# Normalisations written out over one buffer, and one product and one state moved in a state-space scan

## The reference

```python
x = x + _L2_attn_a_ref(_layernorm(x, axis=-1), ...)
x = x + _L2_ffn_ref(_layernorm(x, axis=-1), ...)
```

```python
q = jnp.where(signatures_raw > 0.3, 1.0, jnp.where(signatures_raw < -0.3, -1.0, 0.0))
sigs = signatures_raw + jax.lax.stop_gradient(q - signatures_raw)
cluster_sigs = jnp.sign(sigs.reshape(NUM_CLUSTERS, TPC, D).mean(axis=1))
```

## Time and profile before

| what | value |
|---|---|
| median of three runs | 5309.79 us |
| the profiled execution, its own time | 5316.4 us |
| its span, first to last instruction | 5314.5 us |
| PE, DVE, ACT, POOL busy | 69%, 65%, 44%, 34% |
| mean granted TensorE clock | 0.812 |

### The profile page before, as it was taken

One profiled execution on the slowest core, in us unless ns is written; L12 is line 12 of the kernel. 1 busy time (PEld: TensorE's weight loads), 2 busy tenths in 40 slices (PEclk: granted clock), 3 DMA queues, 4 the chain that ended last, 5 costly groups with the idle time before them and its releaser, 6 DMA issues. The chain is left out here.

```text
span 5314.5 us, 74791 instructions
## 1 busy us (share of the span) xinstructions
PE 3686.4 (69%) x21578; PEld 2430.3 (46%) x21578; DVE 3452.9 (65%) x6649; ACT 2334.0 (44%) x4251; POOL 1781.2 (34%) x1703
## 2 busy tenths in 40 slices
PE   5757566588873568873577777479936949577595
PEld 4657346533322423333422322246634649555494
DVE  4422671379996368854389999668866647656575
ACT  2335324355541347761444444347634526343253
POOL 0043114456661445552234445102220132301423
PEclk9868668789996789995778888679966869778697
DMA  2022002212220232300311111000000012100122
GB/s 96 2 60 78 12 3 83 81 56 64 64 66 13 80 91 88 90 25 28 109 45 49 52 48 56 9 19 1 1 3 2 0 33 61 54 9 0 35 67 61
DMA packets 263352, 238.41 MB, mean 45 GB/s; under 512 B 32713, under 2 KB 217136, under 8 KB 262176
## 3 DMA queue, kind: packets, MB, share of 16 engines
q1 hardware_dynamic: 242592, 193.03, 12.1%
q0 software_dynamic: 20480, 41.98, 2.5%
HBM read 159.06 MB, written 74.97 MB: 44 GB/s over the span
## 5 line engine op out<-in xcount | busy, mean ns | idle before, releaser
L1987 DVE TENSOR_TENSOR_SCAN s_l_attn_a_h<-s_l_attn_a_da,XN 128x512 f32<-128x512 f32 x512 | 598.3, 1210 | 54.9 <-issue 35.3
L1937 ACT ACTIVATE s_l_attn_a_da<-s_l_attn_a_delta,s_l_attn_a_a 128x510 f32<-128x510 f32 x512 | 346.2, 686 | 557.6 <-DVE s_l_attn_a_h L1987 554.3
L1929 PE MATMUL s_l_attn_a_y_ps<-XN,c_ident 128*128 128x512 f32 x1024 | 552.9, 664 | 36.5 <-DVE s_l_attn_a_y L2259 28.9
L611 POOL DMA_INDIRECT s_l_ffn_ffn_back<-slots_y,s_l_ffn_ffn_slots x320 | 304.5, 952 | 515.7 <-DMA slots_y<-PICK 259.8
L507 DVE COPY s_l_ffn_ffn_xt<-s_l_ffn_ffn_turned 128x128 f32<-128x128 f32 x416 | 120.3, 290 | 534.8 <-PE s_l_ffn_ffn_turned L663 532.8
L603 POOL DMA_INDIRECT slots_x<-XN,s_l_ffn_ffn_slots x320 | 309.7, 968 | 451.9 <-DVE s_l_ffn_ffn_slots L482 213.1
L438 ACT COPY s_l_ffn_ffn_own_w<-up 128x512 f32 (+2 forms) x416 | 304.9, 734 | 297.8 <-DVE s_l_ffn_ffn_expert_no L491 193.2
L1947 POOL TENSOR_TENSOR XN<-s_l_attn_a_h,LOG 128x512 f32<-128x512 f32 x256 | 319.8, 1272 | 316.3 <-DVE s_l_attn_a_h L1987 299.8
L674 PE MATMUL s_l_ffn_ffn_up<-s_l_ffn_ffn_xt,s_l_ffn_ffn_own_w 128*128 128x128 f32 x2944 | 412.6, 281 | 6.5 <-DVE s_l_ffn_ffn_shifted_a L515 5.4
L682 PE MATMUL s_l_ffn_ffn_down<-down,s_l_ffn_ffn_hid 128*128 x2944 | 407.4, 279 | 12.9 <-DVE s_l_ffn_ffn_hid L520 6.0
L1947 POOL TENSOR_TENSOR XN<-s_l_attn_a_h,s_l_attn_a_more_c_rows 128x512 f32<-128x512 f32 x256 | 321.0, 1275 | 250.9 <-DVE s_l_attn_a_h L1987 158.2
(11 more groups left out here) (655 smaller groups left out, 8259.7 us busy)
## 6 DMA issues: line engine op xcount, KB each, us to landing
LOG<-s_l_attn_a_c_kept SPq DMA_DIRECT2D x128, 256.0 KB, 3.1
s_l_attn_a_more_c_rows<-s_l_attn_a_c_kept SPq DMA_DIRECT2D x128, 256.0 KB, 3.1
XNT<-slots_x SPq DMA_DIRECT2D x64, 320.0 KB, 5.0
slots_y<-LOG SPq DMA_DIRECT2D x16, 640.0 KB, 4.4
slots_y<-PICK SPq DMA_DIRECT2D x16, 640.0 KB, 4.4
s_l_attn_b_qr<-s_l_attn_b_q_rows SPq DMA_DIRECT2D x64, 144.0 KB
s_l_attn_b_kr<-s_l_attn_b_k_rows SPq DMA_DIRECT2D x64, 144.0 KB
XNT<-slots_x SPq DMA_DIRECT2D x16, 384.0 KB, 4.9
```

Source lines behind the costliest of these rows:

```text
L611: nc.gpsimd.indirect_dma_start(back[:, n % 8, :], None, k.slots_y[h][0:NH * P, :], bass.IndirectOffsetOnAxis(slots[:, c, t:t + 1], 0)).the ...
L1929: last = self.nc.tensor.matmul(self.y_ps[:, i, :], self.k.ident[:], self.hc[n % 2][:, i, :], start=(n == 0 and not begun), stop=(n == NST ...
L1937: self.nc.scalar.activation(self.da_half(g, n, i)[:, :, 1:], self.delta[par][:, i, :].rearrange("p (b t) -> p b t", b=BPG)[:, :, 1:], ACT. ...
L1987: self.nc.vector.tensor_tensor_scan(self.h[n % 2][:, i, :], self.da_half(g, n, i).rearrange("p b t -> p (b t)"), self.u[n % 2][:, i, :], 0 ...
```

## The change

- **Normalisation.** All loops are written out. VectorE writes rows directly into `XN`, so that neither a ring nor GpSimd's copy is needed. ScalarE makes one copy per group, to `XNT`, and the projection reads its weights there. There are three `turned` banks (and three `proj` banks for 72 columns). TensorE's order becomes turn(g+2), project(g). With 8 columns the logits of four groups share a bank and are copied at once. Where statistics are still to be taken, the work goes in three chunks of 8, 8 and 16 tiles. ScalarE loads the table that the next block needs at g = 2.
- **Signatures.** `SIG` is built once, in the first block of the program.
- **Scan of layer 2.** `spread_lam` is one product of two rows: the tile `lam` gets a second row of ones. `project_dt` goes from 12 to 11, `spread_mean` and `move_c` from 14 to 13, `keep_ssm` from 11 to 10, `keep_z` from 12 to 11, `sizes` from 14 to 12, `log_term` from 15 to 14.

```diff
 def load_all(nc, k, weights):
+        raw, q, low = s.sb("raw", [P, NT]), s.sb("q", [P, NT]), s.sb("low", [P, NT])
             sp.dma_start(k.X[:], k.dram["x"]).then_inc(loaded, 16)
+            sp.dma_start(raw[:], k.dram["L2f_sig"]).then_inc(sig_loaded, 16)
...
+            dve.wait_ge(sig_loaded, 16)
+            nc.vector.tensor_scalar(q[:], raw[:], 0.3, None, ALU.is_gt)
...
+            def normalise(g):
+                for t in range(g * GT, (g + 1) * GT):
+                    last = nc.vector.tensor_scalar(k.XN[:, t, :], k.X[:, t, :], meanvar[:, t, 0:1], rstd[:, t:t + 1], ALU.subtract, ALU.mult)
+                last.then_inc(rows_ready, 1)
+            if stats_taken:
+                find_moments(0)
+                invert(0)
+                for g in range(GROUPS):
+                    normalise(g)
+            else:
+                take(0, 2 * GT)
+                find_moments(0)
+                take(2 * GT, 4 * GT)
+                find_moments(1)
+                invert(0)
+                normalise(0)
+                normalise(1)
+                take(4 * GT, 6 * GT)
+                invert(1)
+                normalise(2)
+                take(6 * GT, TILES)
+                find_moments(2)
+                normalise(3)
+                invert(2)
+                for g in range(4, GROUPS):
+                    normalise(g)
...
+            turn(0)
+            turn(1)
+            for g in range(GROUPS):
+                if g + 2 < GROUPS:
+                    turn(g + 2)
                 if project is not None:
+                    project_rows(g)
...
+            for g in range(GROUPS):
+                act.wait_ge(turned_ready, g + 1)
+                nc.scalar.copy(k.XNT[:, g * GROUP:(g + 1) * GROUP], turned[g % 3][:]).then_inc(cols_ready, 1)
+                if g == 1 and len(chunks) == 3:
+                    root(2)
+                if g == 2 and project is not None:
+                    nc.scalar.preload_act_table_set("sigmoid_and_others" if wide else "natural_log_exp_and_others")
...
 def l2_attn_a
             def spread_lam(q):
-                nc.tensor.matmul(aux[:, 0, :], half_row[LAM:LAM + 1, :], k.ones[LAM:LAM + 1, 0:1].to_broadcast([1, GROUP]), start=True, stop=False)
-                nc.tensor.matmul(aux[:, 0, :], half_row[LAM:LAM + 1, :], lam[LAM:LAM + 1, :], start=False, stop=True).then_inc(lam_up, 1)
+                nc.tensor.matmul(aux[:, 0, :], half_row[LAM:LAM + 2, :], lam[LAM:LAM + 2, :], start=True, stop=True).then_inc(lam_up, 1)
...
-                    if n == 12 and r < GROUPS:
+                    if n == 11 and r < GROUPS:
                         project_dt(r)
-                    if n == 14:
+                    if n == 13:
                         if r < GROUPS:
                             spread_mean(r)
                         move_c(q)
...
+            nc.gpsimd.memset(lam[LAM:LAM + 2, :], 1.0)
...
-                        if n == 12:
+                        if n == 11:
                             keep_z(q)
                     if r < GROUPS:
-                        if n == 11:
+                        if n == 10:
                             keep_ssm(r)
+                        if n == 12:
+                            sizes(r)
                         if n == 14:
-                            sizes(r)
-                        if n == 15:
                             log_term(r)
...
 def l2_ffn
-    with Scope(nc, name + "_sig") as s:
...
-            sp.dma_start(raw[:], k.dram["L2f_sig"]).then_inc(loaded, 16)
...
-    layer_norm(nc, k, name + "_ln", k.SIG, NS, keep_rows=True)
+    layer_norm(nc, k, name + "_ln", k.SIG, NS)
```

More of the change, by code:

```diff
@@ L200, in _, with take, find_moments @@
         def _(dve):
-            if not stats_taken:
-                for t in range(TILES):
+            def take(first, last):
+                for t in range(first, last):
                     nc.vector.bn_stats(stats[:, t, :], k.X[:, t, :])
+            def find_moments(c):
+                some = slice(*chunks[c])
                 dve.drain()
-            nc.vector.tensor_tensor(meanvar[:, :, 0], stats[:, :, 1], stats[:, :, 4], ALU.add)
-            nc.vector.tensor_tensor(half_gap[:], stats[:, :, 1], stats[:, :, 4], ALU.subtract)
@@ L233, in layer_norm @@
-        if keep_rows:
-            @block.gpsimd
-            def _(pool):
-                pool.sem_inc(rows_kept, 2)
-                with pool.Fori(0, GROUPS // 2) as pair:
-                    for i in range(2):
-                        pool.wait_ge(rows_ready, pair * 2 + (i + 1))
-                        nc.gpsimd.tensor_copy(k.XN[:, bass.ds(pair * 2 * GT + i * GT, GT), :], rows[i][:]).then_inc(rows_kept, 1)
+                nc.vector.tensor_tensor(meanvar[:, some, 0], stats[:, some, 1], stats[:, some, 4], ALU.add)
@@ new lines, in project_rows @@
+            def project_rows(g):
+                pe.wait_ge(cols_ready, g + 1)
+                if wide and g >= 3:
+                    pe.wait_ge(logits_kept, g - 2)
+                for j in range(GT):
+                    t = g * GT + j
+                    if wide:
+                        out = proj[g % 3][:, j * n_out:(j + 1) * n_out]
+                    else:
+                        out = proj[g // 4][:, (t % 16) * n_out:(t % 16 + 1) * n_out]
+                    last = nc.tensor.matmul(out, k.XNT[:, t * P:(t + 1) * P], project[:, 0:n_out], start=True, stop=True)
+                if wide or g % 4 == 3:
+                    last.then_inc(proj_ready, 1)
@@ new lines, in root, with keep_logits @@
+            def root(c):
+                act.wait_ge(moments, c + 1)
+                nc.scalar.activation(rstd[:, slice(*chunks[c])], rstd[:, slice(*chunks[c])], ACT.Sqrt).then_inc(ready, 1)
+            def keep_logits(n, count):
+                act.wait_ge(proj_ready, n + 1)
+                nc.scalar.copy(k.LOG[:, n * count:(n + 1) * count, 0:n_out],
+                               proj[n % len(proj)][:, 0:count * n_out].rearrange("p (t n) -> p t n", n=n_out)).then_inc(logits_kept, 1)
+            for c in range(min(2, len(chunks))):
+                root(c)
@@ L289, in keep_best_two @@
+            if wide:
+                keep_logits(GROUPS - 1, GT)
+            elif project is not None:
+                keep_logits(1, 4 * GT)
 def keep_best_two(nc, dve, s, values, best, early, keep):
```

153 lines of the change are left out of this document (55 added, 98 removed).

## The result

| | before | after |
|---|---|---|
| median (runs) | 5306.83 us (4) | 5240.38 us (4) |
| lowest to highest | 5302.6 to 5316.52 | 5234.18 to 5249.06 |
| the profiled execution, its own time | 5316.4 | 5242.22 |
| its span | 5314.5 | 5240.4 |

The ratio is 0.9873 with a 95% interval of 0.9853 to 0.9894. The change is faster by 66.4 us, where 35.2 were forecast, and 5240.4 lies outside the range of 5256 to 5296. Whether it is faster was called rightly; how much was wrong by nearly a factor of two.

A forecast was written before the change was run, and what follows sets the result against it. The prediction took TensorE to bound router normalisations and VectorE to bound attention normalisations, and looked at VectorE's waits in the scan. Its terms summed to -35.2 us, from the median of 5309.8 to 5274.6 us, range 5256 to 5296.

The forecast's parts named there:

- Attention with statistics, -6.6: Normalisations s2, s4, s6, s14: ring stops and loop set-up go, 1.65 us each, nothing in s8; 6.6 us faster.
- Attention without statistics, +1.2: Normalisations s0, s10, s12: chunks add chains and reciprocals and buy nothing, 0.4 us each; 1.2 us slower.
- Routers, -1.8: Normalisations s1, s5, s7: TensorE's last group of instructions ends sooner, 0.8 us in s1, 0.6 elsewhere; 1.8 us faster.
- without statistics, -0.9: Router normalisations s3, s13, s15: TensorE's order gives away what the chunks win; 0.9 us faster in all.
- The wide ones, -9.1: s9 and s11: the signature block of 3.95 us goes and TensorE gives 0.6 us; 9.1 us faster for both.
- the load, +0.5: First block: the signatures' load costs an issue and bytes on a queue, between 0 and 1, taken as 0.5 us slower.
- third rival: Normalisations run at the full clock: 5257 us if only s9 and s11, 5205 if all eight; chance 0.06.
- The scan, -17.4: Scan: six spread-product waits go (14.5 us), four short `multiply_cb` waits (1.0), one product at the start (1.9).
- The merged product's 1.9: Scan's start: one lambda product instead of two shortens the wait before the first scan by 1.9 us (0 to 2).
- Rival 1: Scan: the spread-product wait moves instead of going, so the 14.5 us stay; 5289.1 us, chance 0.15.
- Rival 4: Scan falls to the slow clock and TensorE becomes the bound; slower, 5332 us, chance 0.05.
- second rival: Normalisation blocks: written-out code costs at fetch, 1.3 us per block, gain falls by 21 to 5295.4 us; chance 0.13.

The follow-up runs named there:

- e9_unroll: Kernel before with only the four loops over pairs of groups in its normalisations written out; 5336.7 us against 5362.5, ratio 0.9953.
- e6_ring: Changed kernel with VectorE again waiting, before group g of tiles, for the transposes of group g-2; 5319.3 us, ratio 0.9906 to the kernel before.
- e5_one: Changed kernel with one chunk of statistics everywhere, all taken first; ratios to the kernel before 0.9868, 0.987 and 0.9865 in three sets.
- e4_order: Changed kernel with TensorE's old order in the normalisations, two groups of transposes then their two projections; 5304.3 us, ratio 0.9882 to the kernel before.
- e10_order2: Changed kernel with chunks kept, but TensorE projecting group g before turning group g+2; 5300.4 us, ratio 0.9885 to the kernel before.
- e3_sig: Kernel before with only the signatures made once beside the load; 5300.5 us, ratio 0.9984.
- e8_pos: Changed kernel with the scan's six steps back in their old states, one lambda product kept; 5248.1 us, ratio 0.9897 to the kernel before.
- e1_scan: Kernel before with the scan's edits alone; 5294.6 us against 5308.4, ratio 0.9979.
- e2_norms: Kernel before with the rewritten normalisation only, old signatures and scan; 5261.1 us, ratio 0.9909.

## Why the prediction was wrong

**Attention with statistics, -6.6.** Right in mechanism, too small: 14.30 to 11.61 is 2.7 us in s2, not 1.65, and s2, s4, s6 and s14 gave 10.2 us together. Three steps failed. "It makes eight tiles in 2.18 us (0.2725 us each)" counts the last tile's end with every eight; the pitch is 0.259, and 32 x 0.0135 is 0.4 us. "This tail of 1.95 stays" was wrong: it is 1.34 with the clock up, and 1.79 where the clock stays at 0.50 (s12 of the changed kernel), so most of that gain is TensorE's clock. And the stops of 0.42 us, taken off rightly, were put down to the ring alone, where e9_unroll and e6_ring show that nearly half of each was the loop. "In s8 it is worth nothing" failed too: the next block starts 19.2 us after the normalisation's start instead of 20.3, and the last weight load is issued 14.4 us after it instead of 15.0. VectorE waits longer for the weights (8.9 us instead of 7.4), and 1.0 us is left.

**Attention without statistics, +1.2.** Wrong sign: s0, s10 and s12 are 1.2, 1.2 and 0.2 us shorter. The chunks' own price was right (e5_one: 2.0 to 2.4 us; the working had two more chains and two more reciprocals, 2.5). What is set against it was not, in three ways. The working took s12 for all three: from the first statistic to the last tile 18.65 us pass there, but 19.4 in s0 and 19.2 in s10, where the first pass through the loop has pauses like the one shown above. Its sum for afterwards, 19.1, is 18.6 in s12, by smaller chains, reciprocals and tiles. And it has no tail, which is 1.34 instead of 1.95 where the clock rises. Writing the loops out alone gives 2.1 in s0, 2.2 in s10 and 1.7 in s12 (e9_unroll).

**Routers, -1.8, and without statistics, -0.9.** s1, s5 and s7 gave 2.2, 1.7 and 2.3 us, s3, s13 and s15 1.9, 1.1 and 1.7. The step that failed is "then has 92 instructions without a pause, to 281.7": the rate of 0.222 per instruction contained a pause of each pair, when TensorE waits for the copied columns. In s1 of the changed kernel twelve instructions take 2.46 us, 0.205 each. Of the 2.2 us in s1 0.65 is the loop (e9_unroll) and 0.8 the order (e4_order); the other 0.7 wasn't taken apart. The table loaded early gave what was forecast: the exponential starts 1.26 us after the last copy instead of 1.56 in s1, s3, s5 and s7, 1.2 us for 1.1. "What the chunks win, TensorE's order gives away" held: turning the order over gives 1.7 us more (e10_order2).

**The wide ones, -9.1, and the load, +0.5.** The signatures gave 7.9 for 7.4 (e3_sig). "And TensorE gives 0.6 as above" failed: s9 is 17.0 instead of 20.3 to 27.3 us. That is the forecast's third rival, given 0.06, in s9 surely and in s11 perhaps; the six routers of 8 columns stay at 0.50 or 0.51 in the changed kernel.

**The scan, -17.4.** 12.2 (e8_pos) to 12.8 us (e1_scan's groups) for 14.5 + 1.0; 2.8 to 3.4 us are left, as waits up to 0.9 in the first trace and up to 1.7 in two more, which "so all six waits go" denied. The merged product's 1.9 could not be seen: it was read from a wait of 11.7 us that is 9.6 in the second trace of the same kernel. Rival 1 didn't come: ScalarE's waits are 12.1 us against 11.8. Rival 4 neither: the clock between the first and the eighth `multiply_cb` is 0.85, before 0.83.

**Written-out code.** The second rival had 0.13. e9_unroll shows the opposite sign: written-out code is 26 us faster. This is the largest missing term, and the main step that failed: the forecast gave the loops 0.4 us in an attention normalisation, as the gap before the first tile, and took every stop and rate behind it for the buffer's or the engine's own. The forecast named the evidence, "unexplained idle of 0.49 to 0.95 us" at the loops' beginnings, and used it as an argument for a loss. The Trainium skill ("Runtime: NRT & Kernel Launch", "Instruction fetch mechanics") spoke for straight code, and e9_unroll agrees in direction; whether instruction fetch is what the loops cost, no run shows.

**The sum.** By kind, e2_norms against either trace of the kernel before: 11.0 us in s2, s4, s6 and s14, 6.4 in s1, s5 and s7, 4.9 in s3, s13 and s15, 2.7 in s0, s10 and s12, 5 or 14 in s9 and s11, as one takes the second or the first trace, and 1.1 in s8 by the start of its next block: 31 to 41 of 47.3. The rest, 7 to 16 us, is not settled. Part of it may lie in the blocks of unchanged code behind the normalisations: s14's is 247 us on average over the kernels with the new code against 251 in the four traces with the old, s0's, s4's and s10's 1 to 2 us less each, but s2's, s6's and s11's about 1 us longer each. They scatter by up to 10 us from kernel to kernel (s14's from 241 to 251, 244 in e9_unroll), so this is a reading of averages.

## What to carry to other kernels

A wait inside a hardware loop is not all the buffer's: unroll the loop and nothing else before pricing a ring. Here that one edit gave 26 us (18 to 32), more than any buffer or order, where the whole change gave 66; part of it came through TensorE's clock, which a stage with the slow clock throughout tells apart. Take an instruction's rate from a long group without a pause, and look in it for pauses that the next edit removes; and before reading a difference of 5 us between two traces, take a second trace of the same kernel, since the granted clock alone moved s9, s11 and the scan's start by 15 us between two of them. Pieces that overlap nothing (the chunks in attention) cost their full chains, even inside a rewrite that wins.

## What the runs showed of the hardware

A stop of VectorE for another engine, at the same semaphores and with TensorE at its slow clock both times, took 0.42 us in a hardware loop and 0.22 to 0.23 in written-out code, and the start of a loop 0.4 us on VectorE. The tail of an attention normalisation behind the last tile was 1.79 us at a granted clock of 0.50 (s12) and 1.34 where the clock had risen. Identical instructions of s9 took 20.3, 24.4 and 27.3 us at granted clocks of 0.72, 0.56 and 0.53, in the first two cases in one and the same program. The router normalisations s1, s5 and s7, with TensorE busy some 20.4 of 24 us, stayed at 0.50 or 0.51 in every trace, and s15 did in all but the three of e5_one's kernel (0.56 there), while the wide s9 with as many instructions went up to 0.80; the Trainium skill's rule that activity releases the throttle ("TensorE: Matmul & The Clock Gate", "What's actually happening") agrees with s9 and not with the routers.
